# One exponential per key tile over two neighbouring score banks of PSUM

## The chip, the cores and the metric

The kernel runs on one core of a Trainium2 chip. The metric is the time of one execution on the device in microseconds (us); the median of three runs of the kernel before is 1814.85 us. Engines are named as in the profile: PE (TensorE), PEld (its weight loads, which overlap its matmuls), DVE (VectorE), ACT (ScalarE), POOL (GpSimd) and SP (SyncE, which issues DMAs).

## What is computed

Masked self-attention with a residual. `x` is (16, 512, 1024): 16 batches, 512 channels, 1024 tokens; the mask keeps about half of the tokens of a batch.

```python
xt = jnp.transpose(x, (0, 2, 1))
q = xt @ Wq.T                                   # 8 heads of 64 channels
scores = scale * jnp.einsum('bhqd,bhkd->bhqk', qh, qh)   # queries, keys, values are all q
logits = (scores * cmask + (1.0 - cmask) * NEG) * rmask
attn = jax.nn.softmax(logits, axis=-1)
ctx = jnp.einsum('bhqk,bhkd->bhqd', attn, qh)
out = x + transpose(ctx @ Wo.T)
```

A token that the mask drops takes the mean over all tokens in place of attention.

## The kernel before

The kernel sorts each batch's tokens so that those that the mask keeps come first (gathers and scatters on POOL's DMA queue), and computes attention for them alone. With this data the "small" form runs: 5 key tiles (`NT`) of 108 tokens (`R`), so 540 token columns (`C`), taken as two halves of 270 columns (`H`). There are 16 batches of 8 heads, and each head is 5 steps, one per key tile: 640 steps. I number a step by its head `h` and key tile `k`, and count all of them by `n`.

Keys lie on the partitions and queries along the columns. What PE does in one step is written out by hand in `batch` (L1184), and this is also the order in which PE's queue runs it:

1. `max_scores` (L1026): one matmul of 108 keys by 270 queries for the head two further on; DVE's `reduce_max` (L828) takes its maximum. Two banks are used in turn, so each of these matmuls waits (`mx_red`) until the reduce of the matmul two back is done.
2. `scores` (L1029): two matmuls at L1041, one for each half of the queries (I call them first and second), and then two at L1044 that add the low parts and the row maxima to the same banks.
3. `misc`, part 0: a share of the projections, value transposes and output products that a table assigns to the step; in about a third of the steps it is empty.
4. `max_scores` again, for the other half.
5. In step k = 2: the row sums of the head before (L1145) and its ten products with the values (`times_values`, L1054), each two passes in the trace.
6. `misc`, part 1.

ACT's queue holds in every step two exponentials (L698), one for each half: it reads a bank of scores and writes the half `Pt[..., half, :]` in SBUF. Each adds 1 to the semaphore `exp_done`, and each waits for its own matmul of L1044 (`s_ready`). Behind them in the queue come the copies and casts of that step's `misc` work. POOL adds up the tiles of `Pt` (L540) after both halves, and `times_values` reads them on PE.

The scores have three banks of PSUM, used in turn over the halves: half number u = 2n + half takes bank u mod 3. A matmul at L1041 may only start when the exponential of the half that used its bank before, u - 3, is done. For the first matmul of step n that is the second exponential of step n - 2; for the second matmul it is the first exponential of step n - 1 (L1039 and L1040). `at_least` (L221) is a wait that is left out where nothing is to be waited for.

Of the kernel before, what the change touches and what calls it, by code (L numbers as in the profile page):

```python
# [19 lines left out]
P = 128  # L20
# [211 lines left out]
def attention_kernel(nc, x_rows, mask_t, wq, wqT, woT, out_rows, B, T, D):  # L232
# [6 lines left out]
    with ExitStack() as ctx:  # L239
# [3 lines left out]
        def psum(name, shape, dt):  # L243
            return ctx.enter_context(nc.psum_tensor(name, shape, dt))
# [2 lines left out]
            return ctx.enter_context(nc.semaphore(name))  # L247


        ST = [psum(f"scores{i}", [P, 512], F32) for i in range(3)]  # L250
        MX = [psum(f"max_scores{i}", [P, 512], F32) for i in range(2)]
        CT = psum("ctx_psum", [P, 512], F32)
        MB = [psum(f"misc{i}", [P, 512], F32) for i in range(2)]
# [201 lines left out]
        def _(pool):  # L455
# [14 lines left out]
            def body(f, t, plan):  # L470
# [59 lines left out]
                def add_tile(s, h, k):  # L530

                    acc, p0 = t["Pacc"][:R, h % f.NA], (NT * h + k) % f.NP
                    if k == 1:
                        at_least(pool, l_ready, s - f.NA + 1)
                        other = t["Pt"][:R, (NT * h) % f.NP]
                    else:
                        pool.wait_ge(pacc_step, (NT - 1) * s + k - 1)
                        other = acc
                    pool.wait_ge(exp_done, 2 * (NT * s + k) + 2)
                    nc.gpsimd.tensor_tensor(acc, other, t["Pt"][:R, p0], ALU.add).then_inc(pacc_step, 1)  # L540

                pool.wait_ge(idx_made, 1)
# [45 lines left out]
        def _(act):  # L588
            act.wait_ge(consts_made, 8)
            def body(f, t, plan):  # L590
# [90 lines left out]
                def batch(b, par, table, has_prev, has_next):  # L681
                    for h in range(HEADS):
                        s = HEADS * b + h
                        for k in range(NT):
                            if k == 1 and not f.split and (h > 0 or has_prev):
                                keep_ctx(s - 1, h - 1)
                            n = NT * s + k
                            if h == 0 and k == 0:
                                act.wait_ge(mask_step, 3 * (b + 1))

                            at_least(act, pv_done, n - f.NP + 1)
                            ko, so = k - f.NP, s
                            while ko < 0:
                                ko, so = ko + NT, so - 1
                            at_least(act, pacc_step, (NT - 1) * so + max(ko, 1))
                            for half in range(2):
                                act.wait_ge(s_ready, 2 * n + half + 1)
                                nc.scalar.activation(t["Pt"][:R, (NT * h + k) % f.NP, half, :],  # L698
                                                     ST[(2 * (NT * h + k) + half) % 3][:R, 0:H], ACT.Exp,
                                                     bias=t["kbias"][:R, par, k:k + 1],  # L700
                                                     scale=SCALE).then_inc(exp_done, 1)
                            for name, arg, bank, before in table[h, k]:
                                if name == "L":
                                    keep_sums(s - 1, bank)
# [25 lines left out]
        def _(dve):  # L730
# [4 lines left out]
            dve.wait_ge(consts_made, 8)  # L735
            nc.vector.tensor_copy(identR[:], ident[:]).then_inc(consts_cast, 1)
            dve.wait_ge(counted, 1)
            nc.vector.tensor_copy(cnt[:].rearrange("p t b -> p (t b)"), ST[0][:, 0:TT * B]).then_inc(pos_step, 1)
            nc.vector.tensor_copy(n_all[:], ST[1][:, 0:B]).then_inc(pos_step, 1)
            dve.wait_ge(pos_step, 3)  # L740

            nc.vector.tensor_tensor(behind[:], tokid[:], cnt[:], ALU.subtract).then_inc(pos_step, 1)
# [13 lines left out]
            def body(f, t, plan):  # L756
# [32 lines left out]
                for tt in range(TT):  # L789
                    nc.vector.tensor_tensor(t["hot_row"][:, tt, 1:], t["rowno"][:].unsqueeze(1).to_broadcast([P, B - 1, R]),  # L790
                                            t["jl"][:, tt, 1:].unsqueeze(2).to_broadcast([P, B - 1, R]),
                                            ALU.is_equal).then_inc(onehots_made, 1)
                    if tt == 0:
                        dve.wait_ge(perm_made, 1)
                        nc.vector.tensor_tensor(t["idx"][:R, 0], ST[0][:R, 0:NTALL], t["boff"][:R, 0],
                                                ALU.add).then_inc(idx_made, 1)

                def masks(b, par):

                    n = n_all[:, bass.ds(b, 1)]  # L800
                    j = t["jidx"][:, 0:NT]

                    at_least(dve, exp_done, 2 * NT * HEADS * (b - 1))
                    at_least(dve, out_done, NT * (b - 1))
                    nc.vector.tensor_scalar(t["valid"][:, par, :], j, n, None, ALU.is_lt).then_inc(mask_step, 1)
                    nc.vector.tensor_scalar(t["inv"][:, par, :], j, n, None, ALU.is_ge).then_inc(mask_step, 1)
                    nc.vector.tensor_scalar(t["kbias"][:, par, :], j, n, NEG, ALU.is_ge, ALU.mult).then_inc(mask_step, 1)
                    dve.wait_ge(mask_step, 3 * (b + 1))
# [95 lines left out]
                def finish_tile(b, par, k, bank):  # L904
# [12 lines left out]
                masks(0, 0)  # L917
                dve.wait_ge(perm_made, B)
                nc.vector.tensor_tensor(t["idx"][:R, 1:],
                                        ST[2][:R, NTALL:B * NTALL].rearrange("p (b i) -> p b i", b=B - 1),  # L920
                                        t["boff"][:R, 1:], ALU.add).then_inc(idx_made, 1)
                quarter = -(-(NTALL - 1) // 4)
                for name, arg, bank, before in plan[0]:
# [47 lines left out]
        def _(pe):  # L971
# [2 lines left out]
            pe.wait_ge(mask_cast, 1)  # L974
            for tt in range(TT):
                for u in range(tt + 1):
                    nc.tensor.matmul(ST[0][:, B * tt:B * tt + B], tri[:] if u == tt else ones_b[:], mask_b[:, u, :],
                                     start=(u == 0), stop=(u == tt))
            for u in range(TT):
                last = nc.tensor.matmul(ST[1][:, 0:B], ones_b[:], mask_b[:, u, :], start=(u == 0), stop=(u == TT - 1))  # L980
            last.then_inc(counted, 1)

            def body(f, t, plan):
# [7 lines left out]
                    last.then_inc(perm_made, 1)  # L991

                pe.wait_ge(onehots_made, 2)
                order(0, ST[0], slice(0, NTALL))

                pe.wait_ge(loaded, 48)
                for k in range(KD):
# [7 lines left out]
                group = next(n for n in (5, 3, 2, 1) if (B - 1) % n == 0)  # L1005
                with pe.Fori(0, (B - 1) // group) as g:
                    for i in range(1, group + 1):
                        order(g * group + i, ST[2], bass.ds((g * group + i) * NTALL, NTALL))
                pe.wait_ge(g_kept, KD)

                def tile_cols(i):
# [17 lines left out]
                def scores(s, s2, h, k):  # L1029

                    ops = t["ops"][:, h % SLOTS]
                    if k == 0:
                        pe.wait_ge(mrow_put[h % 2], 16 * (s2 + 1))
                    banks, count = [], 2 * NT * HEADS
                    for half in range(2):
                        u = 2 * (NT * h + k) + half
                        banks.append(ST[u % 3])

                        last_user = u - 3 if u >= 3 else next(v for v in range(-1, -4, -1) if (count + v - u) % 3 == 0)  # L1039
                        at_least(pe, exp_done, 2 * NT * (s - h) + last_user + 1)  # L1040
                        nc.tensor.matmul(banks[half][:R, 0:H], ops[:, OPA, tile_cols(k)], ops[:, OPB, half_cols(half)],  # L1041
                                         start=True, stop=False)
                    for half in range(2):
                        nc.tensor.matmul(banks[half][:R, 0:H], ops[:, OPY, tile_cols(k)], ops[:, OPX, half_cols(half)],  # L1044
                                         start=False, stop=True).then_inc(s_ready, 1)

                def times_values(s, p, h, k):

                    if k == 0:
                        at_least(pe, ctx_done if f.split else ct_kept, s)  # L1050
                        at_least(pe, v_kept, 2 * p + 2)
                    for half in range(2):
                        pe.wait_ge(exp_done, 2 * (NT * s + k) + half + 1)
                        last = nc.tensor.matmul(CT[DK * half:DK * half + DK, 0:H],  # L1054
                                                t["V"][:R, (h // 2) % 2, k, DK * (h % 2):DK * (h % 2) + DK],
                                                t["Pt"][:R, (NT * h + k) % f.NP, half, :],
# [185 lines left out]
```

## Time and profile before

| | |
|---|---|
| median of 3 runs | 1814.85 us (1810.24 to 1817.87) |
| the profiled execution | 1814.64 us, its span 1812.8 us |
| PE busy | 1650.4 us (91%), 10956 matmuls |
| DVE busy | 1306.6 us (72%) |
| POOL busy | 1207.7 us (67%) |
| ACT busy | 851.5 us (47%) |
| granted clock of PE, mean | 0.954 |
| ACT's exponentials (L698) | 1280 of 485 ns, 552.9 us in all |
| PE's matmuls of L1041 and L1044 | 2560 of about 0.3 us, spaced 0.12 us |

Matmuls overlap: one of 270 columns is in flight for about 0.29 us, while the next starts 0.12 to 0.13 us after it. So PE's busy time says only that something was in flight, and what a step costs is read from the starts. An entry "x2" in a timeline stands for two instructions that overlap or touch.

### The profile page before, as it was taken

What the parts mean: (1) busy time and instruction counts of PE and PEld (TensorE: products, weight loads), DVE (VectorE), ACT (ScalarE), POOL (GpSimd) and SP (SyncE); (2) the same over time, 40 slices, a digit from 0 to 9 for tenths busy, and PEclk for the clock granted to TensorE, in tenths of its full rate; (3) what the DMA queues carried; (4) which work ended last, traced back from release to release, by engine and by line L of the source; (5) the groups of instructions that cost most, each with busy time, mean ns of one, the idle gap of its engine ahead of it and who ended that gap; (6) DMA issues with size and microseconds to landing.
All of it is one profiled execution on the core that took longest, in us unless ns stands there. A gap on an engine that the chain in (4) does not pass through costs nothing.

```text
span 1812.8 us, 40177 instructions
## 1 busy us (share of the span) xinstructions
PE 1650.4 (91%) x10956; PEld 1260.7 (70%) x10956; DVE 1306.6 (72%) x2839; ACT 851.5 (47%) x2055; POOL 1207.7 (67%) x1030
## 2 busy tenths in 40 slices
PE   6688989999999999989899998999999899999995
PEld 4566767677767777767767777677776677777763
DVE  5358677786857768696776968678685877769663
ACT  1135455454635545364544636445463554546451
POOL 5357776758667675777757677675866767586752
PEclk8689999999999999999999999999999999999997
DMA  3234353434434353443434434253443434344410
GB/s 102 71 83 116 91 129 78 129 80 116 111 87 118 76 135 86 104 121 92 119 71 127 97 103 120 69 137 77 122 102 89 116 81 131 83 117 103 103 48 27
DMA packets 93863, 179.70 MB, mean 99 GB/s; under 512 B 24704, under 2 KB 24832, under 8 KB 93632
## 3 DMA queue, kind: packets, MB, share of 16 engines
q1 hardware_dynamic: 64448, 109.71, 26.4%
q0 software_dynamic: 29184, 67.17, 12.8%
q8 instruction: 113, 1.85, 0.4%
q14 instruction: 118, 0.97, 0.2%
HBM read 36.77 MB, written 33.55 MB: 39 GB/s over the span
## 4 chain that ended last, share of the span: by engine, by line
PE 61%; DVE 23%; issue 10%; POOL 2%; ACT 2%; DVEq 1%; SPq 0%; DMA 0%; ACTq 0%; POOLq 0%
PE misc L1087 19%; PE ctx_psum L1054 12%; PE max_scores L1026 8%; DVE small_mxp L828 8%; PE scores L1041 6%; DVE small_xsum L823 5%; PE scores L1044 5%; DVE small_rsum L858 3%; PE misc L1145 3%; PE misc L1113 3%; DVE small_ctx L879 2%; DVE small_xcT_lo L850 1%; PE misc L1135 1%; PE misc L1099 1%; PE misc L1133 1%
## 5 line engine op out<-in xcount | busy, mean ns | idle before, releaser
L828 DVE TENSOR_REDUCE small_mxp<-max_scores 108x1 f32<-108x270 f32 x1280 | 538.3, 433 | 330.2 <-PE max_scores L1026 299.9
L698 ACT ACTIVATE small_Pt<-scores,small_kbias 108x270 f32<-108x270 f32 x1280 | 552.9, 485 | 451.0 <-PE scores L1044 425.2
L540 POOL TENSOR_TENSOR small_Pacc<-small_Pacc,small_Pt 108x540 f32<-108x540 f32 x384 | 532.1, 1386 | 266.4 <-ACT small_Pt L698 256.5
L1026 PE MATMUL max_scores<-small_ops 128*108 128x270 f32 x1280 | 413.7, 341 | 79.3 <-DVE small_mxp L828 78.4
L1026 PEld LDWEIGHTS max_scores<-small_ops 128*108 128x108 f32 x1280 | 223.8, 178 | 176.2 <-DVE small_mxp L828 110.0
L1054 PE MATMUL ctx_psum<-small_Pt,small_V 108*64 108x270 f32 x2560 | 322.8, 400 | 0.0
L1041 PE MATMUL scores<-small_ops 128*108 128x270 f32 x1280 | 297.4, 305 | 4.8 <-ACT small_Pt L698 3.9
L858 DVE RECIPROCAL small_rsum<-small_rsum 128x67 f32<-128x67 f32 (+1 forms) x512 | 240.5, 530 | 78.3 <-ACT small_rsum L644 78.3
L1044 PE MATMUL scores<-small_ops 128*108 128x270 f32 x1280 | 270.6, 294 | 0.0
L1054 PEld LDWEIGHTS ctx_psum<-small_Pt,small_V 108*64 108x64 f32 x2560 | 190.8, 141 | 113.9 <-issue 10.2
L492 POOL DMA_INDIRECT small_xg<-x_rows,small_idx_cur x160 | 171.1, 1069 | 103.9 <-POOL small_idx_cur L485 63.3
L540 POOL TENSOR_TENSOR small_Pacc<-small_Pt 108x540 f32<-108x540 f32 x128 | 185.2, 1447 | 81.6 <-ACT small_Pt L698 79.8
L1041 PEld LDWEIGHTS scores<-small_ops 128*108 128x108 f32 x1280 | 202.4, 177 | 36.6 <-ACT small_Pt L698 22.6
L499 POOL DMA_INDIRECT out_rows<-small_xg,small_idx_cur x160 | 164.8, 1030 | 74.1 <-DVE small_xg L914 28.5
L1044 PEld LDWEIGHTS scores<-small_ops 128*108 128x108 f32 x1280 | 196.9, 178 | 0.0
L629 ACT CAST small_H<-misc 128x270 fp32r<-128x270 f32 x128 | 49.4, 386 | 229.3 <-PE misc L1087 225.3
L1087 PE MATMUL misc<-small_xcT,small_wqT_hi 128*128 128x270 f32 x512 | 151.3, 295 | 1.8 <-DVE small_xcT_lo L850 1.3
L1087 PE MATMUL misc<-small_xcT_lo,small_wqT_hi 128*128 128x270 f32 x512 | 149.0, 291 | 0.0
L1087 PE MATMUL misc<-small_xcT,small_wqT_lo 128*128 128x270 f32 x512 | 148.6, 290 | 0.0
L510 POOL TENSOR_TENSOR small_xg<-small_xg,small_w 108x512 f32<-108x512 f32 (+1 forms) x80 | 112.7, 1409 | 43.9 <-ACT small_w L618 43.9
L1087 PE MATMUL misc<-small_woT_hi,small_ctxT 128*108 128x512 f32 x320 | 131.9, 412 | 5.0 <-DVE small_ctxT_lo L863 4.9
L823 DVE TENSOR_TENSOR small_xsum<-small_xsum,small_xg 108x512 f32<-108x512 f32 (+1 forms) x128 | 133.9, 1046 | 0.2
(104 smaller groups left out, 2234.0 us busy)
## 6 DMA issues: line engine op xcount, KB each, us to landing
small_ops<-small_H SPq DMA_DIRECT2D x512, 135.0 KB, 2.5
small_ops<-small_L SPq DMA_DIRECT2D x256, 135.0 KB, 2.6
small_xg<-x_rows,small_idx_cur POOLq DMA_INDIRECT x160, 3.6
out_rows<-small_xg,small_idx_cur POOLq DMA_INDIRECT x160, 3.4
small_ops<-small_mrow SPq DMA_DIRECT2D x128, 2.1 KB
wq_sb<-wq SPq DMA_DIRECT2D x1, 1024.0 KB, 5.7
woT_sb<-woT SPq DMA_DIRECT2D x1, 1024.0 KB, 8.2
wqT_sb<-wqT SPq DMA_DIRECT2D x1, 1024.0 KB, 10.2
```

What stands on the lines that cost most here:

```text
L492: nc.gpsimd.indirect_dma_start(out=t["xg"][:r, par, k, :], out_offset=None, in_=x_rows, in_offset=bass.IndirectOffsetOnAxis(ap=t["idx_cur" ...
L499: nc.gpsimd.indirect_dma_start(out=out_rows, in_=t["xg"][:r, par, k, :], in_offset=None, out_offset=bass.IndirectOffsetOnAxis(ap=t["idx_cu ...
L540: nc.gpsimd.tensor_tensor(acc, other, t["Pt"][:R, p0], ALU.add).then_inc(pacc_step, 1)
L698: nc.scalar.activation(t["Pt"][:R, (NT * h + k) % f.NP, half, :], ST[(2 * (NT * h + k) + half) % 3][:R, 0:H], ACT.Exp, bias=t["kbias"][:R, ...
L823: nc.vector.tensor_tensor(acc[:r], other, t["xg"][:r, par, k, :], ALU.add).then_inc(xsum_step, 1)
L828: nc.vector.tensor_reduce(t["mxp"][:R, h % 2, m // 2, m % 2:m % 2 + 1], MX[m % 2][:R, 0:H], AX.X, ALU.max).then_inc(mx_red, 1)
L858: nc.vector.reciprocal(t["rsum"][:, cols], t["rsum"][:, cols]).then_inc(recip_step, 1)
L1026: nc.tensor.matmul(MX[m % 2][:R, 0:H], ops[:, OPA, tile_cols(m // 2)], ops[:, OPB, half_cols(m % 2)], start=True, stop=True).then_inc(mx_r ...
L1041: nc.tensor.matmul(banks[half][:R, 0:H], ops[:, OPA, tile_cols(k)], ops[:, OPB, half_cols(half)], start=True, stop=False)
L1044: nc.tensor.matmul(banks[half][:R, 0:H], ops[:, OPY, tile_cols(k)], ops[:, OPX, half_cols(half)], start=False, stop=True).then_inc(s_ready, 1)
L1054: last = nc.tensor.matmul(CT[DK * half:DK * half + DK, 0:H], t["V"][:R, (h // 2) % 2, k, DK * (h % 2):DK * (h % 2) + DK], t["Pt"][:R, (NT ...
L1087: last = nc.tensor.matmul(out, lefts[a][left_at], rights[z][right_at], start=(c == 0 and i == 0), stop=(c == KD - 1 and i == 2))
```

## The change

The three banks become one tensor `ST` of three neighbouring banks. A key tile takes two neighbouring ones: an even tile banks 0 and 1, an odd tile banks 1 and 2 (`left` is the tile's number mod 2). One activation over both banks, 2 x 270 columns, replaces the two exponentials, and adds 1 to `exp_done`. It waits for both matmuls of L1044. In an odd tile the matmuls for the second half of the queries come first. The matmul that is issued first goes to bank 0 or 2 and waits for the exponential of step n - 2; the one that is issued second goes to bank 1, which every tile uses, and waits for the exponential of step n - 1, all of it. POOL, PE's value products and DVE's `masks` wait for the same tiles as before, counted in tiles in place of halves.

```diff
-        ST = [psum(f"scores{i}", [P, 512], F32) for i in range(3)]
+        ST = psum("scores", [P, 3, 512], F32)
...
-                    pool.wait_ge(exp_done, 2 * (NT * s + k) + 2)
+                    pool.wait_ge(exp_done, NT * s + k + 1)
...
-                            for half in range(2):
-                                act.wait_ge(s_ready, 2 * n + half + 1)
-                                nc.scalar.activation(t["Pt"][:R, (NT * h + k) % f.NP, half, :],
-                                                     ST[(2 * (NT * h + k) + half) % 3][:R, 0:H], ACT.Exp,
-                                                     bias=t["kbias"][:R, par, k:k + 1],
-                                                     scale=SCALE).then_inc(exp_done, 1)
+                            left = (NT * h + k) % 2
+                            act.wait_ge(s_ready, 2 * n + 2)
+                            nc.scalar.activation(t["Pt"][:R, (NT * h + k) % f.NP], ST[:R, left:left + 2, 0:H], ACT.Exp,
+                                                 bias=t["kbias"][:R, par, k:k + 1], scale=SCALE).then_inc(exp_done, 1)
...
-                    banks, count = [], 2 * NT * HEADS
-                    for half in range(2):
-                        u = 2 * (NT * h + k) + half
-                        banks.append(ST[u % 3])
-
-                        last_user = u - 3 if u >= 3 else next(v for v in range(-1, -4, -1) if (count + v - u) % 3 == 0)
-                        at_least(pe, exp_done, 2 * NT * (s - h) + last_user + 1)
-                        nc.tensor.matmul(banks[half][:R, 0:H], ops[:, OPA, tile_cols(k)], ops[:, OPB, half_cols(half)],
-                                         start=True, stop=False)
-                    for half in range(2):
-                        nc.tensor.matmul(banks[half][:R, 0:H], ops[:, OPY, tile_cols(k)], ops[:, OPX, half_cols(half)],
-                                         start=False, stop=True).then_inc(s_ready, 1)
+                    left = (NT * h + k) % 2
+                    order_of_halves = (1, 0) if left else (0, 1)
+                    for i, half in enumerate(order_of_halves):
+                        at_least(pe, exp_done, NT * s + k - 1 + i)
+                        nc.tensor.matmul(ST[:R, left + half, 0:H], ops[:, OPA, tile_cols(k)],
+                                         ops[:, OPB, half_cols(half)], start=True, stop=False)
+                    for half in order_of_halves:
+                        nc.tensor.matmul(ST[:R, left + half, 0:H], ops[:, OPY, tile_cols(k)],
+                                         ops[:, OPX, half_cols(half)], start=False, stop=True).then_inc(s_ready, 1)
...
+                    pe.wait_ge(exp_done, NT * s + k + 1)
                     for half in range(2):
-                        pe.wait_ge(exp_done, 2 * (NT * s + k) + half + 1)
                         last = nc.tensor.matmul(CT[DK * half:DK * half + DK, 0:H],
```

On ACT, at the end of one head and the start of the next (`scores1` is score bank 1, `misc0` a bank of `misc`), the queue before:

```order
L698 ACTIVATE small_Pt<-scores0,small_kbias 108x270 [waits s_ready,pacc_step,pv_done]
L698 ACTIVATE small_Pt<-scores1,small_kbias 108x270 [waits s_ready]
L663 CAST small_ctxT<-small_ctx 128x540 [waits ctx_done]
L698 ACTIVATE small_Pt<-scores2,small_kbias 108x270 [waits s_ready,pacc_step,pv_done]
L698 ACTIVATE small_Pt<-scores0,small_kbias 108x270 [waits s_ready]
L636 COPY small_V<-misc0 108x512 [waits pv_done,v_ready]
```

and after the change:

```order
L698 ACTIVATE small_Pt<-scores,small_kbias 108x540 [waits s_ready,pacc_step,pv_done]
L663 CAST small_ctxT<-small_ctx 128x540 [waits ctx_done]
L698 ACTIVATE small_Pt<-scores,small_kbias 108x540 [waits s_ready,pacc_step,pv_done]
L636 COPY small_V<-misc0 108x512 [waits pv_done,v_ready]
```

Each pair of exponentials has become one instruction of 540 columns, in the same place of the queue. On PE, where a step without `misc` work meets the next one (k = 4 of one head, k = 0 of the next), the queue in the loop body before:

```order
L221 REGISTER_ALU
L1041 MATMUL scores1<-small_ops 108x270 [waits exp_done]
L221 REGISTER_ALU
L1041 MATMUL scores2<-small_ops 108x270 [waits exp_done]
L1044 MATMUL scores1<-small_ops 108x270
L1044 MATMUL scores2<-small_ops 108x270
L221 REGISTER_ALU
L1026 MATMUL max_scores1<-small_ops 108x270 [waits mx_red]
L221 ISA [waits dup1]
L1026 MATMUL max_scores0<-small_ops 108x270 [waits mx_red]
L221 REGISTER_ALU [waits mrow_put1]
L1041 MATMUL scores0<-small_ops 108x270 [waits exp_done]
```

and after:

```order
L1036 MATMUL scores<-small_ops 108x270 [waits exp_done]
L221 REGISTER_ALU
L1036 MATMUL scores<-small_ops 108x270 [waits exp_done]
L1039 MATMUL scores<-small_ops 108x270 x2
L221 REGISTER_ALU
L1024 MATMUL max_scores1<-small_ops 108x270 [waits mx_red]
L221 ISA [waits dup1]
L1024 MATMUL max_scores0<-small_ops 108x270 [waits mx_red]
L221 ISA [waits mrow_put1]
L1036 MATMUL scores<-small_ops 108x270 [waits exp_done] x2
```

No matmul has moved against another (L1036 and L1039 are the former L1041 and L1044); what has changed is which exponential the second wait on `exp_done` stands for, and some register instructions that work out the counts are gone.

## Rows read from the trace of the kernel before

**Rows 1.** The page: span, and busy time of each engine.

```profile
span 1812.8 us, 40177 instructions
PE 1650.4 (91%) x10956; PEld 1260.7 (70%) x10956; DVE 1306.6 (72%) x2839; ACT 851.5 (47%) x2055; POOL 1207.7 (67%) x1030
```

**Rows 2.** The page: the chain that ended last, by engine.

```profile
PE 61%; DVE 23%; issue 10%; POOL 2%; ACT 2%; DVEq 1%; SPq 0%; DMA 0%; ACTq 0%; POOLq 0%
```

**Rows 3.** Waits: who waited <- for whom: us in total, times, longest us.

```profile
ACT small_Pt L698 <- PE scores L1044: 425.2, 269, 4.2
...
DVE small_mxp L828 <- PE max_scores L1026: 299.9, 386, 8.0
...
PEld max_scores L1026 <- DVE small_mxp L828: 110.0, 152, 4.1
...
DVE small_rsum L858 <- ACT small_rsum L644: 78.3, 88, 4.6
```

**Rows 4.** Line L1041, PE and PEld: what its idle engine waited for (us, times).

```profile
  ACT small_Pt L698: 26.5, 107
```

**Rows 5.** Timeline of PE: start us, us, then the instruction; a stretch of short steps.

```profile
1023.21 0.42 PE L1041 MATMUL scores<-small_ops 128*108 128x270 f32 x2
1023.47 0.41 PE L1044 MATMUL scores<-small_ops 128*108 128x270 f32 x2
1023.71 0.62 PE L1026 MATMUL max_scores<-small_ops 128*108 128x270 f32 x2
1024.17 0.53 PE L1041 MATMUL scores<-small_ops 128*108 128x270 f32 x2
1024.54 0.41 PE L1044 MATMUL scores<-small_ops 128*108 128x270 f32 x2
1024.79 0.36 PE L1026 MATMUL max_scores<-small_ops 128*108 128x270 f32 x1
1025.35 0.37 PE L1026 MATMUL max_scores<-small_ops 128*108 128x270 f32 x1 [0.20 <-DVE small_mxp L828]
1025.56 0.41 PE L1041 MATMUL scores<-small_ops 128*108 128x270 f32 x2
```

**Rows 6.** Timeline of ACT in the same stretch.

```profile
1023.79 0.86 ACT L698 ACTIVATE small_Pt<-scores,small_kbias 108x270 f32<-108x270 f32 x2
1024.87 0.86 ACT L698 ACTIVATE small_Pt<-scores,small_kbias 108x270 f32<-108x270 f32 x2 [0.21 <-PE scores L1044]
```

**Rows 7.** Timeline of all engines, last batch, which has no `max_scores`.

```profile
1764.83 0.86 ACT L698 ACTIVATE small_Pt<-scores,small_kbias 108x270 f32<-108x270 f32 x2 [2.32 <-PE scores L1044]
1765.37 0.17 PEld L1041 LDWEIGHTS scores<-small_ops 128*108 128x108 f32 x1 [0.64 <-ACT small_Pt L698]
...
1765.59 0.41 PE L1044 MATMUL scores<-small_ops 128*108 128x270 f32 x2
...
1765.99 0.86 ACT L698 ACTIVATE small_Pt<-scores,small_kbias 108x270 f32<-108x270 f32 x2 [0.30 <-PE scores L1044]
```

**Rows 8.** Groups of ACT by form: busy us, mean ns, then idle before them.

```profile
L698 ACT ACTIVATE small_Pt<-scores,small_kbias 108x270 f32<-108x270 f32 x1280 | 552.9, 485 | 451.0 <-PE scores L1044 425.2 <-POOL small_Pacc L540 16.2 <-issue 0.3
...
L636 ACT COPY small_V<-misc 108x512 f32<-108x512 f32 x64 | 38.3, 598 | 1.6 <-PE misc L1135 1.6
...
L636 ACT COPY small_V<-misc 108x128 f32<-108x128 f32 x64 | 17.1, 266 | 0.0
```

**Rows 9.** Windows: busy us (count) of each engine, granted clock (PEclk), DMA share, GB/s.

```profile
1083.00:1094.00 11.00, 9.51 (x58) 7.83 (x58) 7.26 (x18) 4.61 (x10) 7.43 (x8) 1.00 0.29 86
1094.20:1097.50 3.30, 3.30 (x18) 3.09 (x16) 2.35 (x5) 2.25 (x7) 2.04 (x3) 0.50 0.85 201
```

**Rows 10.** Timeline of PE just ahead of the second of these windows.

```profile
1093.73 0.37 PE L1026 MATMUL max_scores<-small_ops 128*108 128x270 f32 x1 [0.99 <-DVE small_mxp L828]
```

More of the change, by code:

```diff
@@ L737, in _ @@
             dve.wait_ge(counted, 1)
-            nc.vector.tensor_copy(cnt[:].rearrange("p t b -> p (t b)"), ST[0][:, 0:TT * B]).then_inc(pos_step, 1)
-            nc.vector.tensor_copy(n_all[:], ST[1][:, 0:B]).then_inc(pos_step, 1)
+            nc.vector.tensor_copy(cnt[:].rearrange("p t b -> p (t b)"), ST[:, 0, 0:TT * B]).then_inc(pos_step, 1)
+            nc.vector.tensor_copy(n_all[:], ST[:, 1, 0:B]).then_inc(pos_step, 1)
             dve.wait_ge(pos_step, 3)
@@ L794, in body @@
                         dve.wait_ge(perm_made, 1)
-                        nc.vector.tensor_tensor(t["idx"][:R, 0], ST[0][:R, 0:NTALL], t["boff"][:R, 0],
+                        nc.vector.tensor_tensor(t["idx"][:R, 0], ST[:R, 0, 0:NTALL], t["boff"][:R, 0],
                                                 ALU.add).then_inc(idx_made, 1)
@@ L801, in masks @@
                     j = t["jidx"][:, 0:NT]
-                    at_least(dve, exp_done, 2 * NT * HEADS * (b - 1))
+                    at_least(dve, exp_done, NT * HEADS * (b - 1))
                     at_least(dve, out_done, NT * (b - 1))
@@ L919, in body @@
                 nc.vector.tensor_tensor(t["idx"][:R, 1:],
-                                        ST[2][:R, NTALL:B * NTALL].rearrange("p (b i) -> p b i", b=B - 1),
+                                        ST[:R, 2, NTALL:B * NTALL].rearrange("p (b i) -> p b i", b=B - 1),
                                         t["boff"][:R, 1:], ALU.add).then_inc(idx_made, 1)
@@ L976, in _ @@
                 for u in range(tt + 1):
-                    nc.tensor.matmul(ST[0][:, B * tt:B * tt + B], tri[:] if u == tt else ones_b[:], mask_b[:, u, :],
+                    nc.tensor.matmul(ST[:, 0, B * tt:B * tt + B], tri[:] if u == tt else ones_b[:], mask_b[:, u, :],
                                      start=(u == 0), stop=(u == tt))
             for u in range(TT):
-                last = nc.tensor.matmul(ST[1][:, 0:B], ones_b[:], mask_b[:, u, :], start=(u == 0), stop=(u == TT - 1))
+                last = nc.tensor.matmul(ST[:, 1, 0:B], ones_b[:], mask_b[:, u, :], start=(u == 0), stop=(u == TT - 1))
             last.then_inc(counted, 1)
@@ L993, in body @@
                 pe.wait_ge(onehots_made, 2)
-                order(0, ST[0], slice(0, NTALL))
+                order(0, ST[:, 0], slice(0, NTALL))
                 pe.wait_ge(loaded, 48)
@@ L1007, in body @@
                     for i in range(1, group + 1):
-                        order(g * group + i, ST[2], bass.ds((g * group + i) * NTALL, NTALL))
+                        order(g * group + i, ST[:, 2], bass.ds((g * group + i) * NTALL, NTALL))
                 pe.wait_ge(g_kept, KD)
```

## The prediction

> **What bounds the kernel now.** I read the page first. PE is busy 91% of the span, DVE 72%, ACT only 47% [rows 1], and the chain that ended last runs 61% over PE, 23% over DVE and 2% over ACT [rows 2]. So work taken from ACT is worth little by itself: ACT sat idle 425.2 us for scores that PE had not made yet [rows 3]. What matters is how soon ACT hands a bank back to PE. For that I looked at the waits of the matmuls at L1041. They wait for an exponential 107 times, but only 26.5 us in all [rows 4]: the wait is met often and only just. The timelines show where. A step with `misc` work takes PE 1.5 to 7 us and gives ACT ample time. A short one, with no `misc` before the next scores, takes about 1 us: the scores at 1023.21 are followed by those at 1024.17, 0.96 us later, with two `max_scores` between [rows 5]. There the two matmuls of L1041, usually 0.42 us together, take 0.53: the second was held by the first exponential of the step before, which began at 1023.79 [rows 6] and lasted 0.49 us, so until 1024.28.
>
> **The exponential itself.** Two of 485 ns [rows 8] take 0.86 us as a pair, since they overlap by 0.1 us [rows 6]. The trace has none of 540 columns. The lower bound is one of 270, 0.49 us; the upper is the pair, 0.86 us. Between them, the two forms of the copy at L636, out of PSUM and by the same engine, take 598 ns for 512 columns and 266 ns for 128: 332 ns for 384 columns, or 0.865 ns a column [rows 8]. For 270 more columns that is 0.23 us, so I take 0.485 + 0.23, about 0.71 us. ACT saves 0.15 us a step, 640 x 0.15 = 96 us of an engine that is not the bound.
>
> The Trainium skill, page "ScalarE: Activation LUTs", section "What ACT_TABLE_LOAD costs", gives 280 ns plus 0.833 ns a column for an activation whose bias is a column of SBUF. For 270 columns that would be 505 ns where the trace has 485; for 540 it would be 730 ns, an estimate from that page, and the sum below would be 4 us more.
>
> **When a bank comes back.** This is the term that decides. Before, the second matmul of L1041 waits for the first exponential of the step before: that one starts when the first matmul of L1044 is done, and takes 0.49 us. After, it waits for the whole exponential, which starts when the second matmul of L1044 is done, 0.12 us later (two take 0.41 us, one 0.29 [rows 5]), and takes 0.71 us. The bank comes back 0.12 + 0.71 - 0.49 = 0.34 us later. The end of the whole tile, which POOL and the value products wait for, is at 0.12 + 0.71 = 0.83 us where it was 0.86, so nothing changes for them. The first matmul of L1041 still waits for step n - 2, at least a step back, and is free.
>
> The Trainium skill, page "PSUM — Partial Sum Buffer", section "PSUM bank collisions raise a hardware error", asks that access be guarded by bank, not by address: it speaks against a layout in which every tile uses the middle bank. No run here shows what happens without the guard; the kernel keeps it, and its price is the 0.34 us.
>
> The last batch shows the loop bare [rows 7]: the exponential at 1764.83, the weights of the second L1041 at 1765.37 (0.05 us after its end), L1044 at 1765.59, the next exponential at 1765.99. A period of 1.16 us. After, it would be 1.16 + 0.34 = 1.50 us there. In the other batches, where the exponential starts right at its matmul's end, the loop is 0.71 + 0.05 + 0.22 (weights to L1044) + 0.12 + 0.29 = 1.39 us, against short steps of 0.96 us.
>
> **The sum.** The 107 steps in which PE already waits lose the whole 0.34 us: 107 x 0.34 = 36 us. Then there are steps in which the wait is met with less than 0.34 us to spare. I compared in the timelines, step by step, the start of the second weight load of L1041 with the end of that exponential: about 110 more steps are short, by 0.16 us on average, so 18 us; most are steps k = 0 and k = 2, and [rows 5] has the first of such a pair and a near miss. Where a matmul waits anew, its pipeline starts again: the matmul after it comes 0.21 us later in place of 0.12 (1025.35 to 1025.56 [rows 5]), 0.09 us: 110 x 0.09 = 10 us. Together 64 us.
>
> Not all of it reaches the end. In some short steps PE then waits for DVE anyway: after the scores at 1024.54 the weights at 1025.35 come only when DVE's reduce is done, and a delay ahead of it is taken up, as long as DVE is not starved itself. PE's weight loads waited for DVE 152 times, 110.0 us [rows 3]. But DVE waits for `max_scores` 386 times, 299.9 us [rows 3], and there the delay is handed on. As the second is the commoner case, I let a fifth be absorbed: 64 - 13 = 51 us. Against it stand gains too small to take apart: some register instructions less on PE, and 0.15 us less for ACT where it is queued behind a cast. I put them at 0 to 10 us and take 0.
>
> 1814.64 + 51 = 1866 us; the profiled execution and the median of the runs differ by 0.2 us, so this stands for both.
>
> **Rivals.**
>
> *The delay is absorbed: within 0.5% (9 us).* That needs nearly all short steps to be followed by a wait for DVE that has its input already. For it: 110.0 us of such waits, more than the 64 us. Against it: the chain is PE for 61% [rows 2], and after a short step there mostly follows long `misc` work on PE. Time 1820. Chance 5%.
>
> *Faster: ACT's relief counts.* The mechanism is the row sums: DVE waited 88 times for ACT's L644, 78.3 us [rows 3], and that stands behind the exponentials of step k = 2 in ACT's queue. If each of the 128 came 0.15 us earlier and the reciprocals led the chain, that is 19 us; with ACT's other casts perhaps 25. It decides only if the 0.34 us is hidden as in the rival above, that is if the second L1041 has mostly over 0.34 us to spare, against which the 107 waits speak. Time 1814.64 - 20 = 1795. Chance 5%.
>
> *The exponential over two banks costs as two:* 0.86 us. Then a bank is 0.15 us later still in some 220 steps, 33 us, and the time is 1899. Nothing in the trace shows a read that crosses banks. Chance 7%.
>
> *The clock falls too.* PE's granted clock is 1.00 in 1083 to 1094 and 0.50 in the 3.3 us from 1094.2 [rows 9], that is 2.4 and 1.2 GHz, just after PE had stood 0.99 us for DVE [rows 10]. Two to three such stretches stand in each batch. New idle time in the short steps can add one a batch; each doubles 3.3 us of matmul time at most, so 1.7 us lost, 16 x 1.7 = 27 us. Time 1893. Chance 15%. The Trainium skill, page "TensorE: Matmul & The Clock Gate", section "Why this matters for your kernels", warns that idle gaps of this engine bring its clock down; the row agrees in kind, and whether gaps of 0.3 us do it no row shows.
>
> *The change does nothing:* excluded, as the wait for the whole tile and the single activation stand in the queues.
>
> **How the numbers follow.** Forecast 68%: 1866, itself from 1838 (half of the 64 us absorbed and a few us of gain) to 1882 (nothing absorbed). The two slower rivals, 22%, reach to 1899. The range takes the forecast's low side and most of the slower rivals: 1836 to 1896. A measurement of this kernel can tell about 0.5% from no change. Slower by over 0.5%: 68 + 22 = 90%; within 5%; faster 5%.
>
> **What would show it.** Right: activations of 108x540 with a mean near 0.71 us; some 200 or more waits of the former L1041 for ACT, with 60 us or more in all in place of 26.5; short steps of 1.3 to 1.4 us in place of 0.96, and a period near 1.5 us in the last batch; ACT's busy time down by about 96 us to 755; long steps unchanged. Wrong: if PE's waits for DVE shrink by as much as its waits for ACT grow, the delay was absorbed; if the short steps stay at 1 us, the slack was larger than I read; if the mean granted clock drops below 0.95, the clock's rival has a share.

## The result, and the profile after

The changed kernel takes 1868.05 us (median of four runs, 1865.2 to 1868.42) against 1816.15 us of the kernel before, measured beside it: 1.0295 times as long, 95% interval 1.0277 to 1.0313. The forecast was 1866 us. The profiled execution took 1865.2 us, its span is 1863.5 us, 50.7 us longer than before.

The page after, span, busy times and the chain by engine, to be set beside [rows 1] and [rows 2]:

```profile
span 1863.5 us, 37785 instructions
...
PE 1669.4 (90%) x10956; PEld 1259.5 (68%) x10956; DVE 1322.8 (71%) x2839; ACT 775.6 (42%) x1415; POOL 1198.1 (64%) x1030
...
PE 67%; DVE 12%; ACT 8%; issue 8%; POOL 3%; DVEq 1%; SPq 0%; DMA 0%; ACTq 0%; POOLq 0%
```

ACT lost 640 instructions and 75.9 us of busy time, and yet its share of the chain that ended last rose from 2 to 8%. It works less and is waited for more. The exponentials and the waits, in the groups and the list of waits after (the former L1041 is now L1036, L1044 is L1039, L1026 is L1024):

```profile
L698 ACT ACTIVATE small_Pt<-scores,small_kbias 108x540 f32<-108x540 f32 x640 | 454.7, 710 | 574.1 <-PE scores L1039 556.2
```

```profile
ACT small_Pt L698 <- PE scores L1039: 556.2, 446, 4.8
...
DVE small_mxp L826 <- PE max_scores L1024: 328.8, 415, 8.1
...
PEld scores L1036 <- ACT small_Pt L698: 97.9, 212, 1.0
PEld max_scores L1024 <- DVE small_mxp L826: 96.7, 144, 3.1
```

One exponential of 540 columns takes 710 ns. The weight loads of the first score matmuls wait 212 times for it, 97.9 us. The same line's view with PE and PEld together, to be set beside [rows 4] (107 times, 26.5 us):

```profile
  ACT small_Pt L698: 144.8, 371
```

Both these rows count matmuls and weight loads apart, so a step can stand in them twice. Before, the 107 are 94 loads and 13 matmuls, in 89 different steps; after, the 371 are 212 loads and 159 matmuls, in 212 steps.

The waits of the loads of `max_scores` for DVE shrank a little, from 110.0 [rows 3] to 96.7 us, and DVE and ACT themselves wait longer for PE. The same place of the same batch as [rows 5] and [rows 6], PE and then ACT:

```profile
1046.26 0.41 PE L1036 MATMUL scores<-small_ops 128*108 128x270 f32 x2
...
1047.22 0.34 PE L1036 MATMUL scores<-small_ops 128*108 128x270 f32 x1
1047.72 0.38 PE L1036 MATMUL scores<-small_ops 128*108 128x270 f32 x1 [0.16 <-ACT small_Pt L698]
1047.93 0.41 PE L1039 MATMUL scores<-small_ops 128*108 128x270 f32 x2
...
1048.61 0.29 PE L1036 MATMUL scores<-small_ops 128*108 128x270 f32 x1
1049.15 0.37 PE L1036 MATMUL scores<-small_ops 128*108 128x270 f32 x1 [0.25 <-ACT small_Pt L698]
```

```profile
1046.95 0.71 ACT L698 ACTIVATE small_Pt<-scores,small_kbias 108x540 f32<-108x540 f32 x1
1048.38 0.71 ACT L698 ACTIVATE small_Pt<-scores,small_kbias 108x540 f32<-108x540 f32 x1 [0.72 <-PE scores L1039]
```

The pair of score matmuls is torn apart. The first one, into bank 0 or 2, starts on time (1047.22, 0.96 us after 1046.26, as before); the second, into the middle bank, starts 0.50 us after it, 0.06 us after the exponential that began at 1046.95 has ended (1047.66). The next exponential starts 1.43 us after this one, where before it was 1.08 [rows 6].

### The profile page after: what moved, and what is told of

It reads as the page before. It is cut to its first block, busy times and chain, and to the rows that moved or that the text cites. A ratio compares the mean times of both kernels' runs of the same rounds, so it can differ in the third digit from the quotient of the medians.

```text
span 1863.5 us, 37785 instructions
## 1 busy us (share of the span) xinstructions
PE 1669.4 (90%) x10956; PEld 1259.5 (68%) x10956; DVE 1322.8 (71%) x2839; ACT 775.6 (42%) x1415; POOL 1198.1 (64%) x1030
## 4 chain that ended last, share of the span: by engine, by line
PE 67%; DVE 12%; ACT 8%; issue 8%; POOL 3%; DVEq 1%; SPq 0%; DMA 0%; ACTq 0%; POOLq 0%
PE misc L1082 20%; PE ctx_psum L1049 15%; PE scores L1036 8%; PE scores L1039 7%; ACT small_Pt L698 6%; PE max_scores L1024 6%; PE misc L1140 4%; DVE small_mxp L826 4%; PE misc L1108 3%; DVE small_xsum L821 3%; PE misc L1094 2%; POOL small_Pacc L540 1%; PE misc L1130 1%; DVE small_xcT_lo L848 1%; DVE small_rsum L856 1%
## 5 line engine op out<-in xcount | busy, mean ns | idle before, releaser
L698 ACT ACTIVATE small_Pt<-scores,small_kbias 108x540 f32<-108x540 f32 x640 | 454.7, 710 | 574.1 <-PE scores L1039 556.2
L1024 PE MATMUL max_scores<-small_ops 128*108 128x270 f32 x1280 | 408.4, 339 | 67.4 <-DVE small_mxp L826 64.8
L1036 PE MATMUL scores<-small_ops 128*108 128x270 f32 x1280 | 327.3, 311 | 49.6 <-ACT small_Pt L698 46.9
L1024 PEld LDWEIGHTS max_scores<-small_ops 128*108 128x108 f32 x1280 | 223.8, 178 | 158.4 <-DVE small_mxp L826 96.7
L856 DVE RECIPROCAL small_rsum<-small_rsum 128x67 f32<-128x67 f32 (+1 forms) x512 | 240.4, 530 | 83.5 <-ACT small_rsum L644 83.5
L1036 PEld LDWEIGHTS scores<-small_ops 128*108 128x108 f32 x1280 | 208.0, 177 | 108.6 <-ACT small_Pt L698 97.9
L1039 PE MATMUL scores<-small_ops 128*108 128x270 f32 x1280 | 271.7, 294 | 0.0
L492 POOL DMA_INDIRECT small_xg<-x_rows,small_idx_cur x160 | 173.3, 1083 | 103.9 <-POOL small_idx_cur L485 65.1
L1039 PEld LDWEIGHTS scores<-small_ops 128*108 128x108 f32 x1280 | 197.5, 179 | 0.0
L510 POOL TENSOR_TENSOR small_xg<-small_xg,small_w 108x512 f32<-108x512 f32 (+1 forms) x80 | 102.1, 1276 | 42.9 <-ACT small_w L618 42.9
```

Of the source, the lines that this page charges most:

```text
L492: nc.gpsimd.indirect_dma_start(out=t["xg"][:r, par, k, :], out_offset=None, in_=x_rows, in_offset=bass.IndirectOffsetOnAxis(ap=t["idx_cur" ...
L698: nc.scalar.activation(t["Pt"][:R, (NT * h + k) % f.NP], ST[:R, left:left + 2, 0:H], ACT.Exp, bias=t["kbias"][:R, par, k:k + 1], scale=SCA ...
L856: nc.vector.reciprocal(t["rsum"][:, cols], t["rsum"][:, cols]).then_inc(recip_step, 1)
L1024: nc.tensor.matmul(MX[m % 2][:R, 0:H], ops[:, OPA, tile_cols(m // 2)], ops[:, OPB, half_cols(m % 2)], start=True, stop=True).then_inc(mx_r ...
L1036: nc.tensor.matmul(ST[:R, left + half, 0:H], ops[:, OPA, tile_cols(k)], ops[:, OPB, half_cols(half)], start=True, stop=False)
L1039: nc.tensor.matmul(ST[:R, left + half, 0:H], ops[:, OPY, tile_cols(k)], ops[:, OPX, half_cols(half)], start=False, stop=True).then_inc(s_r ...
```

## The experiments

The theory: the bank that the second matmul needs comes back later, because it is released by the end of one long exponential, and that is the whole loss. The rivals: the single exponential itself (its later start, its place in ACT's queue), the new layout and order of the halves, or the clock. The kernel before was measured again beside each group of runs: 1813.4, 1812.7 and 1813.2 us.

**The wait alone.**

```diff
-                        at_least(pe, exp_done, 2 * NT * (s - h) + last_user + 1)
+                        at_least(pe, exp_done, 2 * (NT * s + k) if half else 2 * NT * (s - h) + last_user + 1)
```

> The kernel before, with one wait made longer: the second matmul of L1041 waits for both exponentials of the step before, where it waited for the first. Layout, order and the two exponentials stay as they were. Theory (the bank that comes back late): the pair ends 0.86 - 0.49 = 0.37 us after the first one alone, against 0.34 us in the change, so about the same loss: 1816 + 52 x 0.37 / 0.34 = 1872 us, 1858 to 1884. Rival (the single activation of 540 columns or the new layout costs the time, by its later start or its place in ACT's queue): nothing of that is here, so 1816 us within 5. If both have a share, the time lies between.

1864.44 us against 1813.41, ratio 1.0274 (1.0253 to 1.0296). Nothing of the change is in it but the later release of a bank, and it costs 51 us. In the last batch the pairs of exponentials begin at 1799.52, 1801.05 and 1802.59: a period of 1.53 us, which is 1.16 [rows 7] and the 0.37 us of delay. The waits look like those of the change:

```profile
PEld scores L1041 <- ACT small_Pt L698: 104.3, 219, 1.0
```

**The layout with two exponentials.** The changed kernel, with

```diff
+                            for i, half in enumerate((1 - left, left)):
+                                act.wait_ge(s_ready, 2 * n + i + 1)
+                                nc.scalar.activation(t["Pt"][:R, (NT * h + k) % f.NP, half, :], ST[:R, left + half, 0:H],
...
-                        at_least(pe, exp_done, NT * s + k - 1 + i)
+                        at_least(pe, exp_done, 2 * (NT * s + k) - 2 + i)
...
-                    for half in order_of_halves:
+                    for half in reversed(order_of_halves):
```

> The changed kernel with its bank layout and its order of halves, but two exponentials of 270 columns again, the one over the shared middle bank first; its second pair of score matmuls is issued middle bank first to match, and the second matmul of the first pair waits for that first exponential alone. Theory: the middle bank comes back as early as before, so 1816 us, 1808 to 1826, and the waits of the score matmuls for ACT are back near 26 us. Rival (the pairs of banks or the alternating order cost the time): 1850 us or more.

1811.3 us, ratio 0.9992 (0.9977 to 1.0006). Neither the pairs of banks nor the alternating order costs anything; with the middle bank emptied first, the loss is gone, and the loads' waits are short again. Those of the kernel before, then those of this run:

```profile
PEld scores L1041 <- ACT small_Pt L698: 22.6, 94, 0.7
```

```profile
PEld scores L1038 <- ACT small_Pt L699: 16.6, 70, 0.7
```

**One exponential where there is time for it.** In the same kernel, the steps that no short step follows (24 of 40 in the first 15 batches) have the single exponential, which adds 2 to `exp_done`:

```diff
+TWO_EXPS_AT = [(7, 4), (0, 0), (0, 1), (0, 4), (1, 0), (1, 1), (2, 1), (2, 4), (4, 4), (5, 0), (5, 1), (5, 4), (6, 0), (6, 1),
+               (6, 4), (7, 0)]
...
+                            if f.split and has_next and (h, k) not in TWO_EXPS_AT:
+                                act.wait_ge(s_ready, 2 * n + 2)
```

> The changed kernel's layout. In the steps that are followed by a short step (16 of the 40 of each batch, and all of the last batch) two exponentials, shared bank first, as in the run with two exponentials; in the others one exponential over both banks. Theory: a late bank costs nothing in a long step, so the loss is gone, and what ACT saves in the others brings a few us: 1808 us, 1798 to 1818. Rival (the single activation costs wherever it stands): a share of the 52 us stays in proportion to its 360 of 640 steps, 1845 us.

1810.51 us, ratio 0.9975 (0.9960 to 0.9989). Of 640 tiles, 360 have the single exponential:

```profile
L701 ACT ACTIVATE small_Pt<-scores,small_kbias 108x540 f32<-108x540 f32 x360 | 255.8, 710 | 380.3 <-PE scores L1050 350.7 <-POOL small_Pacc L542 22.3 <-issue 5.0
```

and the 29 us are not there that would be their share of the 52 us if the single exponential cost by itself. This run is a quarter of a per cent faster than the kernel before, but it is not told apart from the run before it, which has two exponentials everywhere (0.9960 to 0.9989 against 0.9977 to 1.0006). So it is not shown that what ACT saves brings anything.

**The same exponential with four banks.** To give the scores a fourth bank, another use had to give one up. Three kernels take the maxima over the first half of the queries alone, which leaves out 640 matmuls and 640 reduces and frees a bank: the base, the change, and the change with four banks.

```diff
                 def max_scores(s, s4, h, m):
+                    if m % 2:
+                        return
...
-        ST = psum("scores", [P, 3, 512], F32)
+        ST = psum("scores", [P, 4, 512], F32)
...
-                            left = (NT * h + k) % 2
+                            left = 2 * ((NT * h + k) % 2)
...
-                    order_of_halves = (1, 0) if left else (0, 1)
+                    order_of_halves = (0, 1)
...
-                        at_least(pe, exp_done, NT * s + k - 1 + i)
+                        at_least(pe, exp_done, NT * s + k - 1)
```

> The kernel before with less work, as the base of the next two runs: the row maxima are taken over the first half of the queries alone, so 640 matmuls of L1026 and 640 reduces of L828 are left out, and the maxima need one bank of PSUM in place of two. DVE loses 640 x 0.43 = 275 us of work and PE 640 x 0.12 = 79 us. Expected 1720 us, 1690 to 1760: PE's part at least, and some of PE's waits for DVE.

> The changed kernel (one exponential per tile, three banks, the middle one used by all tiles) with the same half of the maxima left out as in the run before it, with one bank for them. Theory: short steps are shorter still in this base (one matmul less between the scores), so the late bank costs at least what it costs with all maxima: 50 to 85 us over the base of half maxima. Rival (it is DVE's or ACT's queue that the single exponential disturbs): with DVE relieved, less than 25 us over the base.

> As the run before it, but the bank that the maxima gave up goes to the scores: four banks, so an even tile has banks 0 and 1, an odd tile banks 2 and 3, and both matmuls of L1036 wait only for the exponential of step n - 2. The single exponential of 540 columns, its start and its place are the same. Theory (the shared middle bank is the whole loss): the loss is gone, 0 to 15 us below the base of half maxima. Rival (the single exponential itself, later at its start, costs): the loss stays as with three banks.

Measured: 1764.21, 1831.82 and 1742.14 us; the single runs of each lie within 9 us and do not overlap. The base is 44 us slower than I expected of it: the 79 us of PE that I subtracted were not all on the path. Over the base, the change costs 67.6 us, as the theory has it. With four banks it is 22.1 us faster than the base, more than the 15 us I gave as the most. PE and PEld idle for ACT at the first score matmuls, in the base, the change, and the change with four banks:

```profile
  ACT small_Pt L698: 47.1, 172
```

```profile
  ACT small_Pt L698: 197.7, 433
```

```profile
  ACT small_Pt L698: 2.1, 5
```

```profile
L698 ACT ACTIVATE small_Pt<-scores,small_kbias 108x540 f32<-108x540 f32 x640 | 455.3, 712 | 469.6 <-PE scores L1042 400.0 <-issue 50.0 <-POOL small_Pacc L540 5.9
```

The last row is of the run with four banks: the exponential is the same 0.71 us. What differs from the run with three banks is which banks a tile uses, and with them the order of the halves in odd tiles, which cost nothing in the run with two exponentials; and the loss turns into a gain. Why the gain exceeds 15 us I take from the first of these rows: the base itself waited for exponentials, 47.1 us with PE and PEld together, and that goes too. The split of the 22 us was not measured.

**The halves in turn.** If a bank's return sets the short steps, an earlier return should make the kernel before faster.

```diff
                         nc.tensor.matmul(banks[half][:R, 0:H], ops[:, OPA, tile_cols(k)], ops[:, OPB, half_cols(half)],
                                          start=True, stop=False)
-                    for half in range(2):
                         nc.tensor.matmul(banks[half][:R, 0:H], ops[:, OPY, tile_cols(k)], ops[:, OPX, half_cols(half)],
```

> The kernel before, with its four score matmuls in another order: both of the first half, then both of the second, in place of L1041, L1041, L1044, L1044. So the first exponential need not stand behind the second L1041, the one that waits for a bank, and starts 0.12 us earlier where nothing waits. Theory (a bank's return sets the short steps): the bank comes back 0.12 us or more earlier, most of the 26.5 us of waits for the exponential go, and a few us more in restarts: 1803 us, 1792 to 1811; in the last batch the period falls below 1.16 us. Rival (DVE's reduces or PE's own queue set the short steps, and a bank's return does not): 1816 us within 5.

A miss: 1827.94 us, ratio 1.0068 (1.0045 to 1.0092). The waits for the exponential did go (4.1 us, 14 times, of 26.5), and in the last batch the period fell from 1.16 to 0.76 us, where the exponentials of the first halves begin at 1774.71 and 1775.47. But step (7, 0) began 1.08 us later than before after step (6, 3) in 13 batches, and that is 14 us. I followed DVE back from there. DVE, then POOL, in this run:

```profile
1033.78 0.68 DVE L823 TENSOR_TENSOR small_xsum<-small_xsum,small_xg 108x512 f32<-108x512 f32 x1
...
1034.72 1.77 DVE L823 TENSOR_TENSOR small_xsum<-small_xsum,small_xg 108x512 f32<-108x512 f32 x1
```

```profile
1034.61 1.33 POOL L540 TENSOR_TENSOR small_Pacc<-small_Pt 108x540 f32<-108x540 f32 x1 [0.88 <-ACT small_Pt L698]
```

and in the kernel before:

```profile
1027.06 0.68 DVE L823 TENSOR_TENSOR small_xsum<-small_xsum,small_xg 108x512 f32<-108x512 f32 x1
```

```profile
1027.07 1.86 POOL L540 TENSOR_TENSOR small_Pacc<-small_Pt 108x540 f32<-108x540 f32 x1 [1.00 <-ACT small_Pt L698]
```

The same addition of tokens on DVE takes 0.68 us when it starts first, and POOL's then takes 1.86 in place of 1.33. When the earlier exponential lets POOL start 0.11 us ahead, DVE's takes 1.77. The Trainium skill, page "SBUF — State Buffer", section "Who interferes with whom", says that a DVE instruction with two inputs in SBUF contends with a POOL instruction that reads SBUF, and that the order of issue decides who blocks. That the two contend, the trace agrees; that the earlier start wins, it shows here but not everywhere. In ten batches of the kernel before, another of these additions starts 0.62 us ahead of POOL's and yet is the one that is held. DVE, then POOL:

```profile
682.84 2.53 DVE L823 TENSOR_TENSOR small_xsum<-small_xsum,small_xg 108x512 f32<-108x512 f32 x1
```

```profile
682.29 1.15 POOL L492 DMA_INDIRECT small_xg<-x_rows,small_idx_cur  x1 [0.30 <-issue]
683.46 1.35 POOL L540 TENSOR_TENSOR small_Pacc<-small_Pt 108x540 f32<-108x540 f32 x1
```

There POOL was in a gather (L492) when DVE's addition began, and its own addition followed 0.02 us behind the gather. No run tested whether the gather decides it.

**POOL held back.** The halves in turn, and in `add_tile`

```diff
+                    if f.split and has_next and (h, k) == (6, 1):
+                        pool.wait_ge(xsum_step, (NTALL - 1) * (b + 1) + 8)
```

> The run with the halves in turn, plus one wait on POOL: in step (6, 1) of each batch its addition of two tiles of exponentials (L540) starts only after DVE's addition of tokens (L823) that falls in that step. The run with the halves in turn came out at 1828 us, and there this token addition took 1.77 us in place of 0.68, because POOL's addition began 0.11 us ahead of it, where before it began 0.01 us after it. Theory (two additions that read SBUF on DVE and POOL block each other, and the first one there goes first): the token addition is back at 0.68 us, 14 x 1.1 = 15 us come back, and what the bank's earlier return gives shows: 1811 us, 1800 to 1816. Rival (the new order of matmuls costs the time on PE itself): 1828 us within 5.

1820.1 us, ratio 1.0027 (1.0005 to 1.0050): 8 of the 15 us. That addition is back at 0.68 us in every usual batch, but the next one, until then 1.47 us, went to 1.81, behind POOL's delayed one. So the next run holds POOL past both, and past two in head 5, with `(h, k) in ((5, 1), (6, 1))` and `{5: 5, 6: 9}[h]` in place of 8.

> The run with the halves in turn, with POOL's additions held back further: in step (5, 1) until the second of DVE's token additions of head 5, in step (6, 1) until both of the token additions that follow (the last one included). Holding only past the first one gave 8 of the 15 us that were expected, since the last token addition went from 1.47 to 1.81 us, behind POOL's delayed one. Theory (the two engines' additions block each other): the last token addition falls to 0.62 us and the second of head 5 from 1.47 to 0.62, 14 x (1.2 + 0.85) = 29 us less on DVE, of which I expect half on the path: 1805 us, 1795 to 1815. Rival: POOL's sums now come late to the row sums, or the order of the halves itself is what costs: 1820 us or more.

1807.73 us, ratio 0.9969 (0.9945 to 0.9993). DVE's token additions, in the run with the halves in turn and in this one:

```profile
L823 DVE TENSOR_TENSOR small_xsum<-small_xsum,small_xg 108x512 f32<-108x512 f32 (+1 forms) x128 | 149.7, 1169 | 0.2
```

```profile
L825 DVE TENSOR_TENSOR small_xsum<-small_xsum,small_xg 108x512 f32<-108x512 f32 (+1 forms) x128 | 114.9, 898 | 0.2
```

These additions take 34.8 us less (all of DVE 31.6 us less, 1305.3 in place of 1336.9), and the run is 20 us shorter in all. To see whether this is a gain of the holds alone, they were also put into the kernel before and into the kernel with one exponential in the long steps.

> The run with one exponential in the long steps, plus the same two holds on POOL (heads 5 and 6). It stood at 1811 us, with token additions of 1.47 us where the holds should give 0.62: 14 x 1.7 = 24 us less on DVE, half of it on the path: 1798 us, 1788 to 1808. Rival (DVE has slack there): 1811 us within 5.

> The kernel before, plus the same two holds on POOL and nothing else, to tell what they give by themselves: 1801 us, 1790 to 1811, by the same count (1.47 to 0.62 us at two token additions a batch, half of it on the path). Rival (DVE has slack there): 1814 us within 5.

Both misses: 1810.9 us (ratio 0.9979, 0.9956 to 1.0002) and 1813.82 us (ratio 0.9998, 0.9971 to 1.0025). In the second, the additions fell from 133.9 to 114.0 us,

```profile
L825 DVE TENSOR_TENSOR small_xsum<-small_xsum,small_xg 108x512 f32<-108x512 f32 (+1 forms) x128 | 114.0, 891 | 0.2
```

and the time did not move: there, DVE had the slack. So the holds only take back what the collision cost, and the 5 us by which the last run of the halves in turn is faster than the kernel before come from the order of the halves, if from anything; its interval nearly reaches 1. A second collision is still in that run: in step (3, 0) of six batches DVE's product that was L914 takes 2.1 us or more in place of 0.75, and the step is 1.3 to 2.0 us longer. No run holds POOL back there, so what the order of the halves is worth without it is open. This run is the fastest version that computes everything, by a third of a per cent, and not told apart from the one with single exponentials in long steps (0.9975).

## Why the prediction was right

*The exponential.* 0.71 us was expected and 710 ns measured. The rival in which two banks cost as two is out. The exponentials occupy ACT for 454.7 us in place of 552.9 [rows 8], 98.2 us less where 96 were expected. ACT's whole busy time fell by 75.9 us only: before, exponentials overlapped with ACT's other instructions for 49.8 us in all, after the change for 25.9 us. The sign that I gave, 96 us less on all of ACT, left this out; nothing hung on it.

*The bank's return.* The decisive term, 0.34 us, shows in the last batch, where nothing else is in the way. I forecast a period of 1.50 us for 1.16 [rows 7]:

```profile
1799.62 0.71 ACT L698 ACTIVATE small_Pt<-scores,small_kbias 108x540 f32<-108x540 f32 x1 [2.66 <-PE scores L1039]
1801.13 0.71 ACT L698 ACTIVATE small_Pt<-scores,small_kbias 108x540 f32<-108x540 f32 x1 [0.79 <-PE scores L1039]
1802.64 0.71 ACT L698 ACTIVATE small_Pt<-scores,small_kbias 108x540 f32<-108x540 f32 x1 [0.80 <-PE scores L1039]
```

It is 1.51, and 1.53 in the run with the wait alone, whose delay is 0.37. Over the whole trace I compared the start of the second score matmul in each step. Of the 639 distances, 198 were below 1.34 us before; they went from 1.10 to 1.40 us on average, 59.6 us together. The other 441 gave 7.1 us back. Before, 163 distances were below 1.2 us, after, none.

*The sum.* 64 us of delay and a fifth absorbed gave 51 us. Measured over all steps, 59.6 - 7.1 = 52.5 us, and 51.9 us between the medians. The mechanism is right, but that the sum meets the measurement within 1 us is luck, for three reasons. The first term took the 107 waits of [rows 4] for 107 steps, where they are 89. The share that is absorbed was a judgement: the waits of the loads of `max_scores` for DVE are down by 13.3 us, but the gains that I put at 0 are in the same sum. (Nothing absorbed would give 1814.64 + 64 = 1879 us, not 1882.) And a cost that the prediction does not have is in the 52 us. In step (3, 0) of six batches DVE's product, L912 (formerly L914), is now held by POOL, after the change and then before:

```profile
1116.50 2.05 DVE L912 SCALAR_TENSOR_TENSOR small_xg<-small_w,small_inv,small_xsum 108x512 f32<-108x512 f32 x1
```

```profile
1116.65 1.34 POOL L540 TENSOR_TENSOR small_Pacc<-small_Pacc,small_Pt 108x540 f32<-108x540 f32 x1
```

```profile
1090.86 0.75 DVE L914 SCALAR_TENSOR_TENSOR small_xg<-small_w,small_inv,small_xsum 108x512 f32<-108x512 f32 x1
```

```profile
1091.05 1.76 POOL L540 TENSOR_TENSOR small_Pacc<-small_Pacc,small_Pt 108x540 f32<-108x540 f32 x1
```

In these six batches the step is 1.3 to 1.45 us longer, from its first score matmul to that of the next, 8.5 us together. The long steps as a whole still gave the 7.1 us back.

*The rivals.* The delay was not absorbed, and ACT's relief did not count: DVE's waits for the row sums (L858 on L644, now L856) went from 78.3 to 83.5 us. The clock did not fall: the mean granted clock is 0.956 after and 0.954 before, and 0.98 in the window 1000 to 1100 in both. The trace before has 24 half-speed stretches, about 168 us in all, not two to three in each batch, as I had written; the trace after has 26, about 165 us in all. So the 0.1 to 0.3 us of idle time that the short steps gained brought no more time at half speed.

*The cause.* The run with the wait alone has the loss without the single exponential; the runs with two exponentials, with long steps only and with four banks have the layout or the single exponential without the loss. The middle bank that all tiles share is therefore no cost in itself; its late return is. The wait alone costs 51 us without the collision in step (3, 0), with a delay of 0.37 us in place of 0.34. In the change, up to 8.5 of the 52 us come by way of that collision, which the shifted times set off; no run of the change removes it, so its share is not shown.

## What to carry to other kernels

Fusing two instructions over two buffers saves their fixed cost on the engine that runs them, but it also releases both buffers at the end of the longer one; ask first who waits for a buffer, how often it is met with little to spare, and count those places, before counting what the engine saves. If two halves share a ring of three buffers, keep the split where the next user is near, or give the fused form four buffers: here, in kernels that take half of the maxima, the same instruction cost 68 us over its base with three banks and gained 22 us with four. Fusing only where the next user is far cost nothing here, and what it gained could not be told from nothing. And when an edit only shifts times, look at the instruction that became longer, not at the edit: a tenth of a microsecond in the start of one engine's addition was worth 14 us.

## What the runs showed of the hardware

One activation that reads two neighbouring banks, 2 x 270 columns, takes 710 ns, and one of 270 columns 485 ns: 0.83 ns for each further column. That is no more than the 0.865 ns of the copies, which read one bank [rows 8], so the step to the next bank adds nothing that shows. Two separate ones occupy ACT for 0.86 us.

Additions of two SBUF tensors on DVE and POOL hold each other up: 0.68 us against 1.77 on DVE, and 1.33 against 1.86 on POOL. In one step a start 0.1 us earlier decided which one was held. The recorded starts are not the whole rule: at 682.84 DVE's addition began 0.62 us first and took 2.53 us. DVE's product in step (3, 0) began 0.19 us before POOL's addition in the kernel before and 0.15 us before it in the changed one, both times while POOL was in a gather (L492), and took 0.75 and 2.05 us. What decides it is open.

A matmul that had to wait for its bank is 0.38 us long in place of 0.29, and the next one starts 0.21 us after it in place of 0.12 (1047.72 to 1047.93 above).
